# A graph and mixture-of-experts layer on one core: a wait ahead of every eighth row gather, the node stage of five groups moved into the aggregation, and the expert bias moved from the combine stage into the experts

## The chip, the cores and the metric

The kernel runs on one core of one Trainium2 chip. The metric is the device time of one execution in microseconds, as the median of several runs. It is written in Bass: every engine (PE for matmuls, DVE and ACT for elementwise work, POOL = GpSimd, SP = the sync queue) runs its own instruction list, and the lists meet only at semaphores.

## What is computed

`x` has 6250 nodes of 256 features. The kernel pads them to 49 tiles of 128 rows, in 7 groups of 7 tiles.

```python
xn = layernorm(x)
gnn = relu(xn @ W_self + (segment_sum(xn[src], dst) / max(deg, 1)) @ W_neigh + b)   # 100000 edges
mix = (linear_attention(xn) * sigmoid(gelu(norm(xn) @ Wg1 + bg1) @ Wg2 + bg2)) @ Wproj + bproj
x2 = x + gnn + mix
y = layernorm(x2)
h = y @ W_gat                                    # 4 heads x 4 experts
alpha = softmax over the 131072 edges + self loops of a node of leaky_relu(a_src[src] + a_dst[dst])
scores = layernorm(segment_sum(h[src] * alpha) + b_gat).mean(heads)
gate = softmax of the two best of four scores, else 0
out = x2 + sum_e gate[e] * (gelu(y @ W1[e] + b1[e]) @ W2[e] + b2[e])
```

## The kernel before, in words

The program has five stages, each in blocks that end with a meeting of all engines.

`prepare` normalises `x`, writes the table `xn_tab` (rows already multiplied by `W_neigh`) to DRAM, sorts the 100000 edges by target and makes tables that say for each round of the aggregation which target tile it adds to, and how far the gathers must have come.

`aggregate` sums the table rows of each target. POOL issues 784 indirect DMAs at line 857, one per 128 edges: each fetches 128 rows of 1 KB into one slot of a ring `msg` of 4 quarters with 8 slots each. Eight gathers are called a half, and there are 98 halves. POOL makes one stop in each half, ahead of its fifth gather (`u == 4`): it waits until PE has finished with the ring quarter that the next half will overwrite (`t.freed`), and until the whole previous half has landed (`landed`), which it then tells PE through the semaphore `s_landed`. ACT builds one-hot matrices `hot` (`prep`, lines 1301 and 1303). PE multiplies them with the gathered rows into 4 PSUM banks (`steps`, line 1125), two slots a round, and DVE adds each bank to `acc` (`sums`, line 879). Between these rounds the same engines do the attention branch of `mix` (PE lines 1142 to 1196) and sort the 131072 edges of the attention stage (DVE lines 218 to 273). The attention branch writes its result and the self term of `gnn` to DRAM, as `base_d`, two rows of 256 a node. The aggregation has 880 slots in all; the last 144 of them are called `rest(u0, u1)`, in PE's list and in DVE's, and hold no work of `mix` beside them. SP loads the first three groups of `base_d` back (`BASES`) during `rest`.

`gnn_out` begins when the aggregation has ended. For each unit (a group of 7 tiles, or 4 or 3 tiles of one at both ends) DVE divides the sums by the degree and adds the base (`mean`, line 1481), forms `x2` (line 1492) and its moments (lines 1496 and 1499), ACT takes the root and normalises (line 1585), PE transposes the rows (line 1635), ACT copies them out (line 1596), PE multiplies them with `w_gat` (line 1646), and SP stores `x2`, the transposed rows (`x2nT_d`) and the heads' rows (`hx_d`). The keys of the sorted edges are loaded and decoded beside it.

`gat_gather_experts` does two things side by side. POOL issues 648 indirect DMAs (line 1821) that gather the heads' rows of the sorted edges, paced by PE's progress (`paced`), with no stop for landings inside a block of 112. PE runs 4 experts on 7 groups: the first layer (line 1996) into 4 banks, which ACT puts through gelu (line 2061), and the second layer (line 2011) into 2 banks `psY`, two tiles a bank, which ACT copies out (line 2068).

`gat_combine` finds each node's sums by 49 more indirect DMAs (line 2175) and 49 small matmuls (`sel`, line 2190), computes the gates in two parts (tiles 0 to 13, then 14 to 48: `gates_of`), and for each group adds four gated expert rows and a bias: ACT scales two experts' rows (line 2225), DVE does two by a multiply and add (line 2421), adds ACT's two (line 2426), and adds the bias `gates @ b2`, which PE makes from transposed gates (lines 2201 and 2207, copied between by ACT) and DVE reads from PSUM (line 2429).

```python
for h in range(HALVES):                      # line 847, POOL
    q = h % QUART
    for u in range(SHALF):
        if h and u == SHALF // 2:
            if h + 1 in range(QUART, HALVES):
                at = h + 1 - QUART
                pool.wait_ge(s_mm, pool.value_load(t.freed[:, at:at + 1], ...))
            landed(h - 1)
        at = h * SHALF + u
        pool.indirect_dma_start(msg[:, q, u, 0:D], None, c.xn_tab, ...).then_inc(s_g[q], 16)
```

## Time and profile before

| | |
|---|---|
| median of 3 runs | 2260.66 us (2257.95 to 2261.66) |
| span of the profiled execution | 2712.5 us |
| its own time | no other figure of it is given than the span |
| mean granted TensorE clock in it | 0.825 |
| first to last gather of the aggregation (line 857) | 102.8 to 1387.9 us |
| `gnn_out` | about 1415 to 1503 us |
| first to last gather beside the experts (line 1821) | 1503.8 to 2453.3 us |
| `gat_combine` | about 2524 to 2712 us |

The profiled execution is 452 us, or 20%, longer than the median run. A row of the trace is therefore a row of an execution that ran slower than the ones that are timed; where it lost time, and where not, has to be read from the trace before its durations are summed. Times in the trace are microseconds from the start of the span; "idle" is the time an engine stood before an instruction, with what ended it; "issue" means that nothing the profile shows was waited for.

### The profile page before, as it was taken

The page shows a single profiled execution, that of the slowest core. Times are in us where ns is not written, and L with a number is a line of the kernel's source. Part 1 is how long each engine was busy: PE and PEld are TensorE (multiplying, and loading weights), DVE is VectorE, ACT ScalarE, POOL GpSimd, SP SyncE. Part 2 cuts the span into 40 slices and gives each one's busy share as a digit, 9 for nine tenths or more (in the row PEclk, how much of TensorE's full clock was granted, in tenths as well). Part 3 has the DMA queues.
Part 4 walks back from the last instruction along what each step waited for, and adds up shares of the span by engine and source line. Part 5 has one row for each costly group of instructions (what it writes and reads, how often), then busy time and mean ns, then how long its engine had stood idle before and what let it go on. Part 6 is the DMA issues. An engine that isn't in the chain of part 4 may idle for free. (4 is left out here: it accounts for less than half of the span.)

```text
span 2712.5 us, 26680 instructions
## 1 busy us (share of the span) xinstructions
PE 1935.5 (71%) x7528; PEld 1334.5 (49%) x7528; DVE 1195.4 (44%) x2204; ACT 893.4 (33%) x1910; POOL 1474.4 (54%) x1512
## 2 busy tenths in 40 slices
PE   5588778876766776666547788878888788884235
PEld 4454445454544544444336455555555565553223
DVE  6353222344454555443348433324424344256368
ACT  3433345444435343443315211321222213132124
POOL 2456456565656665556630566666666666661510
PEclk8888789887888888777775799998999889897555
DMA  5443222234334433435329511121211212215544
GB/s 182 147 132 123 62 82 86 72 117 135 117 112 130 130 118 105 131 93 179 89 61 296 208 36 50 36 70 36 70 36 50 56 45 61 51 36 172 159 148 152
DMA packets 197044, 282.80 MB, mean 104 GB/s; under 512 B 43024, under 2 KB 147443, under 8 KB 195762
## 3 DMA queue, kind: packets, MB, share of 16 engines
q0 software_dynamic: 61280, 115.13, 15.9%
q1 hardware_dynamic: 97218, 121.11, 13.5%
q10 hardware_dynamic: 38416, 44.96, 5.0%
q8 instruction: 66, 1.08, 0.2%
q14 instruction: 64, 0.52, 0.1%
HBM read 195.29 MB, written 85.80 MB: 104 GB/s over the span
## 5 line engine op out<-in xcount | busy, mean ns | idle before, releaser
L857 POOL DMA_INDIRECT ag_msg<-xn_tab,step_src x784 | 782.1, 998 | 504.9 <-issue 224.0
L1821 POOL DMA_INDIRECT edge_rows<-hx_d,gat_src x648 | 621.2, 959 | 329.6 <-issue 187.4
L1125 PE MATMUL ag_ps<-ag_msg,ag_hot 128*128 x1760 | 494.0, 430 | 113.5 <-issue 67.8
L1125 PEld LDWEIGHTS ag_ps<-ag_msg,ag_hot 128*128 128x128 f32 x1760 | 366.8, 216 | 238.5 <-issue 181.2
L879 DVE TENSOR_TENSOR acc<-acc,ag_ps 128x257 f32 x440 | 186.0, 423 | 671.1 <-remote 329.8
L2011 PE MATMUL ex_psY<-co_rows 128*128 128x256 f32 x1568 | 401.4, 413 | 100.2 <-issue 44.5
L2011 PEld LDWEIGHTS ex_psY<-co_rows 128*128 128x128 f32 x1568 | 320.8, 208 | 175.6 <-issue 68.7
L1996 PE MATMUL ex_psF<-co_rows 128*128 128x448 f32 x896 | 360.7, 557 | 42.8 <-ACT co_rows L2061 16.9
L1301 ACT ACTIVATE gat_self<-iota_row,step_nloc 128x128 f32<-128x128 f32 x880 | 271.4, 388 | 343.3 <-issue 199.1
L1935 DVE TENSOR_TENSOR hi_one_low<-hi_numbers,hi_low 128x2048 bf16<-128x2048 f32 x64 | 146.4, 2287 | 481.3 <-remote 309.5
L1996 PEld LDWEIGHTS ex_psF<-co_rows 128*128 128x128 f32 x896 | 172.2, 196 | 214.5 <-issue 187.6
L2061 ACT ACTIVATE co_rows<-ex_psF,ex_b 128x448 f32<-128x448 f32 x224 | 136.1, 633 | 247.6 <-PE ex_psF L1996 166.6
L2068 ACT COPY co_rows<-ex_psY 128x512 f32<-128x512 f32 x112 | 59.3, 532 | 473.2 <-remote 207.3
L1142 PE MATMUL mx_ps<-wqkv,xnT 128*128 128x512 f32 x196 | 105.1, 663 | 55.7 <-ACT gat_dst L1314 40.5
L1303 ACT ACTIVATE ag_hot<-gat_self,ones 128x1024 f32<-128x1024 f32 x110 | 126.3, 1148 | 13.6 <-issue 6.0
L1194 PE MATMUL mx_ps<-wself,xnT 128*128 128x256 f32 x196 | 62.4, 448 | 83.4 <-DVE xnT L903 55.4
L1936 DVE TENSOR_TENSOR hi_one_high<-hi_numbers,hi_high 128x1568 bf16<-128x1568 f32 x64 | 114.0, 1781 | 0.0
L1194 PEld LDWEIGHTS mx_ps<-wself,xnT 128*128 128x128 f32 x196 | 41.2, 219 | 95.7 <-DVE xnT L903 59.1
L1142 PEld LDWEIGHTS mx_ps<-wqkv,xnT 128*128 128x128 f32 x196 | 40.4, 211 | 89.8 <-issue 44.2
L1312 ACT ACTIVATE gat_dst<-mx_ps 128x256 f32<-128x256 f32 x49 | 18.7, 382 | 190.7 <-PE mx_ps L1145 87.9
L218 DVE TENSOR_TENSOR gatsort_keys<-gatsort_keys 128x512 f32<-128x512 f32 x117 | 80.2, 686 | 1.0
L219 DVE TENSOR_TENSOR gatsort_keys<-gatsort_keys 128x512 f32<-128x512 f32 x117 | 80.1, 685 | 0.0
(377 smaller groups left out, 2004.9 us busy)
## 6 DMA issues: line engine op xcount, KB each, us to landing
y_d<-co_rows ACTq DMA_DIRECT2D x28, 896.0 KB
co_rows<-y_d SPq DMA_DIRECT2D x28, 896.0 KB, 9.5
ag_msg<-xn_tab,step_src POOLq DMA_INDIRECT x784
xnT<-base_d SPq DMA_DIRECT2D x7, 1792.0 KB
edge_rows<-hx_d,gat_src POOLq DMA_INDIRECT x648
base_d<-xnT ACTq DMA_DIRECT2D x7, 1024.0 KB
sums_d<-edge_rows SPq DMA_DIRECT2D x5, 1344.0 KB
xg<-in_x_dram SPq DMA_DIRECT2D x7, 896.0 KB, 6.1
```

The source lines that it names most:

```text
L857: pool.indirect_dma_start(msg[:, q, u, 0:D], None, c.xn_tab, bass.IndirectOffsetOnAxis(ap=t.idx[:, at:at + 1], axis=0)).then_inc(s_g[q], 16)
L879: V.tensor_tensor(own, own, bank[(at // JOIN + u) % BANKS][:, 0:ROWW], ALU.add).then_inc(s_acc, 1)
L1125: last = nc.tensor.matmul(bank[(at + r) % BANKS][:, 0:ROWW], hot[:, k, u0 + r * JOIN + j, :], ring[:, j * ROWW:SLOTS * ROWW][:, ds(places[ ...
L1142: nc.tensor.matmul(b[:, :], xnT[:, k, at:at + P], wqkv[:, k, D:3 * D], start=(k == 0), stop=False, skip_group_check=True)
L1301: A.activation(dif[:, u, :], c.iota_row[:], ACT.Abs, bias=t.nloc[:, ds(half * SHALF + u, 1)])
L1303: A.activation(hot[:, k], dif[:], ACT.Relu, bias=c.ones[:, 0:1], scale=-1.0).then_inc(s_hot, 1)
L1821: pool.indirect_dma_start(G[:, j % RING, w, :], None, c.hx_d, bass.IndirectOffsetOnAxis(ap=plan.idx[:, at + w:at + w + 1], axis=0)).then_i ...
L1935: V.tensor_tensor(one_low[:, k % 2], bcast(numbers, 1, HIST), bcast(low[:, at], 2, P), ALU.is_equal)
L1936: V.tensor_tensor(one_high[:, k % 2], bcast(numbers[:, 0:HIGHS], 1, HIST), bcast(high[:, at], 2, HIGHS), ALU.is_equal).then_inc(s_one, 1)
L1996: last = nc.tensor.matmul(psF[i % FB][:, 0:HB], w1[:, e, k, (i % HC) * P:(i % HC + 1) * P], yT[:, k, (i // HC) * HB:(i // HC + 1) * HB], s ...
L2011: last = nc.tensor.matmul(bank[:, (u - u0) * D:(u - u0 + 1) * D], hh[:, k].rearrange("p a b -> p (a b)")[:, u * P:(u + 1) * P], w2[:, e, k ...
L2061: nc.scalar.activation(hh[:, i % HC, i // HC, :], psF[i % FB][:, 0:HB], ACT.Gelu, bias=b1[:, e * HC + i % HC:e * HC + i % HC + 1]).then_in ...
```

## The change

Four edits.

1. In the aggregation POOL gets a second stop in each half: ahead of the eighth gather it waits until the seven others of this half have landed.
2. A class `NodeRows` holds the work of `gnn_out`. Its units are all 4 or 3 tiles now. Five of the seven groups (10 units, `FUSED = 5`) are done beside `rest`: DVE does `mean` of unit i at slot 60 + 8 i and `moments` four slots later, ACT does `root`, `normed`, `turned` and `headed` between its `prep`s and behind them, PE does `turns` and `heads` between the rounds of `rest(80, ...)`, with the two banks `mix` taken in turn, and SP stores `x2`, the turned rows and the heads and loads the base groups 3 to 6. `x2` is written over `acc`, and the normalised rows over the base. `gnn_out` keeps groups 5 and 6 and the keys.
3. The combine stage computes the gates in three parts (groups 0 and 1, 2 to 4, 5 and 6), and has no transposes of gates, no bias matmuls and no third addition of DVE.
4. The bias goes into the experts instead: `b2` is loaded to all partitions (512 KB), ACT copies it into a bank of `psY` before PE's second layer adds to it, and PE waits for that copy.

```diff
@@ aggregate, SP
+                nodes.load_heads(sp, a)
...
-                    sp.dma_start(base[:, g], rows_v[:, g * GT:(g + 1) * GT, :]).then_inc(c.s_base[g], 16)
+                    nodes.base_in(sp, g)
...
                 sp.dma_start(c.skey_gat[0:P].rearrange("(p j) -> p j", p=1), first[:]).then_inc(s_out, 16)
+                nodes.rows_out(sp, 0)
+                nodes.rows_out(sp, 1)
+                nodes.base_in(sp, 3)
+                nodes.turned_out(sp, 0)
...
                 sp.dma_start(c.skey_gat[P + SORT_N:P + GAT_N].rearrange("(p j) -> p j", p=P), upper[1][:]).then_inc(s_out, 16)
+                nodes.heads_out(sp, 2)
+                nodes.base_in(sp, 6)
+                nodes.turned_out(sp, 3)
+                nodes.rows_out(sp, 4)
+                nodes.heads_out(sp, 3)
+                nodes.turned_out(sp, 4)
@@ aggregate, POOL
                             landed(h - 1)
+                        if u == SHALF - 1:
+
+                            pool.wait_ge(s_g[q], 16 * (SHALF * (h // QUART) + u))
@@ aggregate, DVE
                     sums(at, tiles_of(at, u1 - u0), 0, u1 - u0)
+                    i, begun = divmod(u1 - FINAL, SHALF)
+                    if begun == 0 and 0 <= i < FUSED_UNITS:
+                        nodes.mean(v, i)
+                    elif begun == SHALF // 2 and 0 <= i <= FUSED_UNITS:
+                        if i:
+                            nodes.scales(v, i - 1)
+                        if i < FUSED_UNITS:
+                            nodes.moments(v, i)
@@ aggregate, PE
-                rest(80, 120)
+                rest(80, 92)
+                nodes.turns(pe, 0, 0, KC)
+                rest(92, 96)
+                nodes.turns(pe, 0, KC)
+                rest(96, 104)
+                nodes.heads(pe, 0)
...
-                rest(132, REST)
+                rest(132, 136)
+                nodes.heads(pe, 2)
+                rest(136, 140)
+                nodes.turns(pe, 3, 0, KC)
+                rest(140, REST)
+                nodes.turns(pe, 3, KC)
+                nodes.heads(pe, 3)
+                nodes.turns(pe, 4)
@@ aggregate, ACT
+                    if h >= 2 * S_ITERS - BESIDE:
+                        noded(h - 2 * S_ITERS + BESIDE)
+                for i in range(BESIDE, FUSED_UNITS + 2):
+                    noded(i)
+                nodes.turned(act, FUSED - 1, KC)
@@ NodeRows
+    def base_in(self, sp, g):
+
+        if g >= BASES:
+            sp.wait_ge(self.s_x2, (g - BASES + 1) * GT)
+            sp.wait_ge(self.s_fill, (g - BASES) * self.FILLS + 2 * KC)
+        sp.dma_start(self.base[:, g % BASES], self.base_v[:, g * GT:(g + 1) * GT, :]).then_inc(self.c.s_base[g % BASES], 16)
...
+    def normed(self, act, i):
+
+        g, u0, n = self.unit(i)
+        act.wait_ge(self.s_scale, i + 1)
+        for u in range(u0, u0 + n):
+            self.c.nc.scalar.activation(self.base[:, g % BASES, u, D:2 * D], self.rows[:, g * GT + u, 0:D], ACT.Identity,
+                                        bias=self.shift[:, g % 2, u:u + 1], scale=self.rstd[:, g % 2, u:u + 1]).then_inc(self.s_y, 1)
@@ gat_gather_experts, SP, PE and ACT
+                sp.dma_start(b2[:].rearrange("p e d -> p (e d)"),
+                             a["b2"].rearrange("e d -> (e d)").rearrange("(o n) -> o n", o=1).to_broadcast([P, EXPERTS * D])).then_inc(s_w[0], 16)
...
-                        pe.wait_ge(s_yc, (g * EXPERTS + e) * len(FILLS) + f + 1)
+                        fill = (g * EXPERTS + e) * len(FILLS) + f
+                        pe.wait_ge(s_yc, max(fill + 1, 2 * fill + YB - 2))
...
-                                                        w2[:, e, k, :], start=(k == 0), stop=(k == HC - 1))
+                                                        w2[:, e, k, :], start=False, stop=(k == HC - 1), skip_group_check=True)
...
+                def biased(n, f):
+
+                    m = FILLS[f][1]
+                    nc.scalar.copy(psY[f % YB][:, 0:m * D].rearrange("p (t d) -> p t d", t=m),
+                                   bcast(b2[:, n % EXPERTS], 1, m)).then_inc(s_yc, 1)
...
                         nc.scalar.copy(yo[:, u0:u0 + m, :].rearrange("p t d -> p (t d)"), psY[f % YB][:, 0:m * D]).then_inc(s_yc, 1)
+
+                        act.wait_ge(s_yc, 2 * (n * len(FILLS) + f) + YB + 1)
+                        biased(n + (f + YB) // len(FILLS), (f + YB) % len(FILLS))
@@ gat_combine
-        CUT = 2
-        parts = [slice(0, CUT * GT), slice(CUT * GT, TILES)]
+        CUTS = (0, 2, 5, GROUPS)
+        parts = [slice(a0 * GT, a1 * GT) for a0, a1 in zip(CUTS, CUTS[1:])]
...
-                pe.wait_ge(s_in, 64)
-                for g in range(GROUPS):
-
-                    pe.wait_ge(s_exp_in, 4 if g < CUT else 7)
...
-                    last.then_inc(s_bias, 1)
...
-                        turned_gates(g)
...
                     for e in range(BY_ACT):
                         v.wait_ge(s_term, BY_ACT * g + e + 1)
-                        V.tensor_tensor(rows[EXPERTS], rows[EXPERTS], rows[e], ALU.add)
-                        v.drain()
-                    v.wait_ge(s_bias, g + 1)
-                    V.tensor_tensor(rows[EXPERTS], rows[EXPERTS], ps_b[:, 0:GT * D], ALU.add).then_inc(s_sum, 1)
+                        if e:
+                            v.drain()
+                        last = V.tensor_tensor(rows[EXPERTS], rows[EXPERTS], rows[e], ALU.add)
+                    last.then_inc(s_sum, 1)
```

## Rows read from the trace of the kernel before

**Rows 1.** POOL's three lines of gathers: duration min/median/max in ns, first and last start

```profile
L857 POOL DMA_INDIRECT ag_msg<-xn_tab,step_src x784: 940/946/2322, 102.8 to 1387.9; - x196
...
L1821 POOL DMA_INDIRECT edge_rows<-hx_d,gat_src x648: 938/944/2098, 1503.8 to 2453.3; - x162
...
L2175 POOL DMA_INDIRECT gc_num<-sums_d,gat_endpos x49: 940/944/1084, 2525.1 to 2585.2; - x49
```

**Rows 2.** Windows 2542 to 2601: busy us of each engine, TensorE clock, DMA share, GB/s

```profile
2542.00:2594.00 52.00, 4.91 (x25) 6.43 (x24) 11.55 (x44) 3.46 (x5) 33.45 (x36) 0.50 0.36 100
2594.00:2601.00 7.00, 6.78 (x32) 5.84 (x31) 6.43 (x18) 0.18 (x1) 0.00 (x0) 0.50 0.00 0
```

**Rows 3.** Timeline of 1300 to 1315: start, length, engine, [idle before it]

```profile
1300.41 0.95 POOL L857 DMA_INDIRECT ag_msg<-xn_tab,step_src  x1 [0.30 <-issue]
1301.66 0.95 POOL L857 DMA_INDIRECT ag_msg<-xn_tab,step_src  x1 [0.30 <-issue]
...
1306.48 1.12 POOL L857 DMA_INDIRECT ag_msg<-xn_tab,step_src  x1 [3.87 <-remote]
...
1313.00 0.97 POOL L857 DMA_INDIRECT ag_msg<-xn_tab,step_src  x1 [0.30 <-DMA ag_msg<-xn_tab,step_src]
```

**Rows 4.** Windows around the gather of 1301.66, same columns as rows 2

```profile
1301.66:1302.61 0.95, 0.00 (x0) 0.00 (x0) 0.00 (x0) 0.00 (x0) 0.95 (x1) 0.50 0.44 134
1302.61:1304.10 1.49, 0.00 (x0) 0.00 (x0) 0.00 (x0) 0.00 (x0) 0.00 (x0) 0.50 0.32 91
1304.10:1306.48 2.38, 1.56 (x4) 1.29 (x5) 1.20 (x3) 0.77 (x3) 0.00 (x0) 0.50 0.00 0
```

**Rows 5.** DMA queues of 1251.3 to 1256.2, behind a gather that ended at 1251.23

```profile
DMA packets 841, 1.86 MB, mean 379 GB/s; under 512 B 62, under 2 KB 62, under 8 KB 839
...
q1 hardware_dynamic: 674, 1.35, 75.9%
q0 software_dynamic: 165, 0.48, 27.0%
```

**Rows 6.** Waits of POOL, 200 to 1400: us in total, times, longest

```profile
POOL ag_msg L857 <- PE ag_ps L1125: 207.1, 42, 14.2
POOL ag_msg L857 <- issue: 206.1, 655, 3.8
POOL ag_msg L857 <- remote: 50.7, 16, 4.4
```

**Rows 7.** Windows of the stages from 1239 on, same columns as rows 2

```profile
1239.00:1389.00 150.00, 77.09 (x233) 55.25 (x232) 45.60 (x91) 49.59 (x124) 100.74 (x104) 0.70 0.40 127
...
1389.00:1415.00 26.00, 15.40 (x53) 11.24 (x51) 12.55 (x48) 2.18 (x5) 0.23 (x1) 0.73 0.10 29
1415.00:1503.00 88.00, 54.40 (x294) 52.77 (x294) 67.99 (x237) 42.76 (x94) 1.61 (x3) 0.57 0.75 241
1503.00:1516.00 13.00, 4.56 (x7) 2.35 (x8) 8.14 (x15) 1.12 (x1) 9.94 (x11) 0.51 0.95 322
1516.00:2454.00 938.00, 791.24 (x3444) 534.44 (x3443) 351.38 (x333) 222.51 (x358) 611.45 (x639) 0.92 0.21 57
```

**Rows 8.** Timeline of the first unit of `gnn_out`

```profile
1415.57 1.67 DVE L1481 SCALAR_TENSOR_TENSOR acc<-acc,go_rdeg,xnT 128x256 f32<-128x256 f32 x4
1417.33 1.43 DVE L1492 SCALAR_TENSOR_TENSOR go_x<-acc,xnT 128x256 f32<-128x256 f32 x4
1418.85 1.40 DVE L1496 BATCH_NORM_STATS2 go_stats<-go_x 128x6 f32<-128x256 f32 x4
1420.33 0.38 DVE L1499 BATCH_NORM_AGGREGATE go_mv<-go_stats 128x2 f32<-128x6 f32 x4
```

**Rows 9.** DVE's longest wait in 1415 to 1503, at the end of `gnn_out`

```profile
DVE gs_keep L1890 <- PEq L1431: 14.7, 1, 14.7
```

**Rows 10.** Groups of PE's work in 1420 to 1560: busy us, mean ns, idle

```profile
L1646 PE MATMUL go_psH<-go_wg,go_yT 128*128 128x24 f32 x196 | 34.3, 336 | 8.2 <-ACT go_yT L1596 8.2
...
L1635 PE MATMUL go_psY<-ident,go_y 128*128 128x128 f32 x98 | 21.8, 409 | 22.8 <-DVEq L1540 15.3 <-ACT go_y L1585 7.5
```

**Rows 11.** ACT's copies out of the second layer's banks, and who waited for them

```profile
L2068 ACT COPY co_rows<-ex_psY x112: 372/585/592, 1538.3 to 2464.3; 128x512 f32<-128x512 f32 x84, 128x256 f32<-128x256 f32 x28
...
  PE ex_psY L2011: 40.0, 9
```

**Rows 12.** DVE's bias additions, and pieces of the chain that ended last

```profile
L2429 DVE TENSOR_TENSOR co_rows<-co_rows,co_ps_b x7: 2020/2022/2022, 2609.4 to 2705.8; 128x1792 f32<-128x1792 f32 x7
...
2623.46 0.59 DVEq L2325
...
2647.49 1.67 PE co_ps_gT L2201 x7
2649.20 0.78 issue
```

More of the change, by code:

```diff
@@ L682, with aggregate @@
 CHUNKS = 2 * GROUPS
+FUSED = 5
 REST = S_ITERS * SBLK - 2 * R_PAIR * SBLK
[L686 removed]
+def aggregate(c, a, t, acc, plan, xnT, r2, base, nodes):
     nc = c.nc
@@ L1578, in rows @@
-                def rows(i):
-                    g, u0, n = units[i]
-                    act.wait_ge(s_scale, i + 1)
-                    if g >= 2:
-                        act.wait_ge(s_turn, (g - 1) * TURNS)
-                    for u in range(u0, u0 + n):
-                        A.activation(y[:, g % 2, u, :], x2[:, g % 2, u, :], ACT.Identity, bias=shift[:, g % 2, u:u + 1],
-                                     scale=rstd[:, g % 2, u:u + 1]).then_inc(s_y, 1)
-                def turned(g, first=0, end=TURNS):
-                    if g >= 2 and first == 0:
-                        act.wait_ge(s_yst[g % 2], 16 * (g // 2))
-                        act.wait_ge(s_hx, g - 1)
-                    for j in range(first, end):
-                        (u0, n), k = HALF[j // KC], j % KC
-                        act.wait_ge(s_turn, g * TURNS + j + 1)
-                        A.copy(yT[:, g % 2, k, u0 * P:(u0 + n) * P], psY[j][:, 0:n * P]).then_inc(s_yT, 1)
@@ L1650, in _ @@
-                pe.wait_ge(s_wg, 1)
-                for g in range(GROUPS):
-                    turns(g)
-                    heads(g)
+                nodes.heads(pe, FUSED - 1)
+                for g in range(FUSED, GROUPS):
+                    nodes.turns(pe, g)
+                    nodes.heads(pe, g)
 def gat_gather_experts(c, a, plan, hot, early, far_in):
@@ L2149, in gat_combine @@
         PER = 512 // CAR
-        FIRST = CUT * GT
-        places = [(ps_b, 0, FIRST), (ps_in, FIRST, FIRST + PER), (ps_out, FIRST + PER, TILES)]
+        edges = [0, parts[0].stop, (parts[1].start + parts[1].stop) // 2, parts[1].stop, TILES]
+        places = list(zip(ps_sel, edges, edges[1:]))
+        assert all(t1 - t0 <= PER for _, t0, t1 in places)
         def sel(t):
@@ L2322, in carried @@
                     v.wait_ge(s_sel, i + 1)
-                    for bank, t0, t1 in places[0:1] if i == 0 else places[1:]:
+                    for bank, t0, t1 in places:
+                        if not T.start <= t0 < T.stop:
+                            continue
                         V.tensor_copy(got[:, t0:t1, :], bank[:, 0:(t1 - t0) * CAR].rearrange("p (t r) -> p t r", r=CAR))
@@ L2494, in program @@
         prepare(c, a, t, acc, plan, xnT, r2)
-        aggregate(c, a, t, acc, plan, xnT, r2, base)
-        gnn_out(c, a, acc, plan, base)
+        nodes = NodeRows(c, sb, acc, plan, xnT, base)
+        aggregate(c, a, t, acc, plan, xnT, r2, base, nodes)
+        gnn_out(c, plan, nodes)
     ctx, sb, ps = c.open()
```

437 lines of the change are left out of this document (236 added, 201 removed).

## The prediction

> **What bounds the kernel now.** The first question is what the 452 us are by which the profiled execution is longer than the median. I read the windows first. In the combine stage there is a stretch of 52 us in which POOL gathers, and PE gets 25 small matmuls done; in the 7 us after POOL's last gather it does 32 of the same kind [rows 2]. Nothing in the list makes PE wait for those gathers, and "issue" is all that the trace names. So while gathers run, the profiled execution holds other engines back. I take that as a cost of being profiled, which a timed run hasn't got. Busy shares of the aggregation and the experts are then of little use, and I look for what can't be compressed.
>
> That is POOL's issue of gathers. One takes 0.946 us in the median, in all three stages [rows 1], and the next begins 0.30 us later [rows 3], so 1.25 us each. The three lines hold 784 + 648 + 49 = 1481 gathers: 1851 us. Around them, by their first and last starts [rows 1] and a last length of about 1.3 and 0.9 us, lie 102.8 us ahead of the first, 114.6 between aggregation and experts, 70.9 between experts and combine, and 126.3 behind the last. The sum is 1851 + 415 = 2266 us. The profiled execution itself took 2712.5 us, 447 more, which is POOL waiting or running long in it; but the median of the timed runs is 2260.7, within 6 us of POOL's chain with no wait at all. So my reading is that in the timed runs POOL sets the pace of the aggregation and nearly that of the experts.
>
> How much could be waiting in the runs? Of the 126 us at the end, some 36 are due to the held-back PE (the first two groups' output, 2601 to 2623, and the late selection could run beside the gathers), so about 30 us of POOL waits fit into a timed run. In the profile they are 207 us for PE and 51 for what the trace can't name [rows 6].
>
> **The wait at every eighth gather.** Only POOL's gathers stand behind it, and `landed` of this half, which PE's rounds need. Its price is the time from the end of a gather's instruction to its landing, since the next gather begins 0.30 us after either. The instruction that began at 1301.66 ends at 1302.61 and its queue moves data to 1304.10, then 0 GB/s: 1.49 us at most [rows 4]. That a landing which POOL waits for adds nothing to the 0.30 us is seen at 1313.00 [rows 3]. I take 1.4 us, and 98 halves: +137 us where POOL is the pace. The Trainium skill (Perfetto Trace Analysis, DMA Instruction — SWDGE (GPSIMD)) says that the bar of such an instruction ends when the descriptors are written, and not at the landing; by the window behind 1302.61 [rows 4] the trace agrees, and whoever took the bar's end as the landing would price this edit at 0 and the whole change at 2216 us.
>
> Below, the price is 0: POOL's waits for PE [rows 6] are 207 us, more than 137, and if the timed runs have them too, each new wait only shortens the next old one. I use that as far as the sum leaves room: of the 30 us about 20 are absorbed. Above, landings take longer beside large transfers: for 5 us the other queue holds 76% of the engines' time and the gathers 27% [rows 5]. No row gives a landing alone there; the longest stop not put down to PE is 4.4 us [rows 6], and I take that as the upper end. The aggregation's last 176 us hold 14 halves, and edit 2 puts five stores of `x2`, five of turned rows and three base loads more beside them (some 14 MB; at the 322 GB/s of the busiest window [rows 7], 44 us of full queues). A quarter of 14 halves at 3 us more is +11, all of them is +42. The Trainium skill (DMA: Bandwidth & Descriptors, Latency and other measured facts) gives the latency of HBM as 0.2 us on average and 2 us under high load. By it, an estimate, every half would cost 1.8 us more if the load were high all along, 176 us on top; the window above is at 91 GB/s [rows 4] and shows no such load, so the sum goes by the rows.
>
> This edit: 137 - 20 + 11 = +128, ends 0 and +180.
>
> **Five groups beside the aggregation.** `gnn_out` takes 88 us, with DVE busy 68 [rows 7]. A unit of four tiles costs DVE 1.67 + 1.43 + 1.40 + 0.38 = 4.9 us [rows 8], 1.25 a tile with gaps. For the two groups left, 14 tiles are 17.5 us; keys and probe some 8; and the end behind DVE's last work is 14.7 us [rows 9] and stays. That makes 40, so -48. The 35 other tiles put 44 us on DVE into 150 us where it is busy 46, and on PE 5/7 of 34.3 + 21.8 = 40 us [rows 10] where it is busy 77 of 150 [rows 7]; 35 ACT rows and copies are some 30 us beside its 50. Between gathers at 1.25 us that fits under POOL: 8 slots last 10 us or more, and DVE needs 4.9 for the unit, 1.7 for four sums and 2.8 for two sorting steps. Should that cover go, the excess is about 1 us for each of 10 units. Behind the last gather there are 26 us in which PE does its last rounds [rows 7]. Heads 1 to 3 and turns 2 to 4 stand in PE's list between or behind these, 3 x 4.9 + 3 x 3.1 = 24 us of PE, of which I take 14 as added. SP's queue gets the loads and stores too; base group 6 is asked for only after turns 3, and its 1.8 MB come in 6 us at 322 GB/s, while group 5 is worked on. Together -48 + 14 = -34; ends -48 (all hidden) and -10 (PE's 24 us and DVE's excess exposed).
>
> **Combine.** Seven additions of 2.02 us leave DVE's chain [rows 12], with their drains 14.5 us. The turn of the gates ahead of both parts, 1.67 + 0.78 us on the chain each [rows 12], goes too: 5. A third pass of `gates_of` is added: the second took from 2623.46 to 2647.49 for 35 tiles [rows 12]; its instructions are short, so I put half of a pass down to their number and not to their size: 9 to 12 us. Some 4 us come from parts that needn't wait for all 49 gathers. -13; ends -36 and 0.
>
> **Bias in the experts.** The load of 512 KB ahead of the first weights is 1.6 us at 322 GB/s [rows 7]: +2. ACT's 112 copies at 0.585 us [rows 11] add 65 us to 222 busy of 938 [rows 7], so they are hidden unless PE waits for a bank. A bank holds two tiles of 4 matmuls, and PE fills the other one meanwhile at about 0.4 us a record of which there are 16: longer than two copies. PE waited 40 us for the copy before, in nine places [rows 11]; if each doubles, +20 and up to +40. I take 0 for it. The combine edits don't touch the experts' gathers.
>
> **Sum.** 2260.7 + 128 - 34 - 13 + 2 = 2344 us.
>
> **The rivals.**
> - *POOL's stop is hidden (faster).* In the timed runs PE, ACT and DVE set the pace of the aggregation, as the 207 us [rows 6] say of the profiled one, 2.7 us a half with the 51. For it: these rows. Against it: the sum of 2266 us would be chance. It decides where POOL already waits 1.4 us a half; then 2260.7 - 45 = 2216. At half of that the change comes out near 2280, and it nets nothing where 45 of the 137 us are exposed.
> - *Landings under load.* The node groups' transfers and the new stop meet: +180 in place of +128, 2396 us. For it: the shared queues [rows 5]. Against it: only 14 of 98 halves are there.
> - *The node units are not covered.* DVE or PE becomes the bound of `rest`, because turns wait for ACT's rows, those for DVE, and rounds stand behind them in PE's list: +24 on the forecast, 2368.
> - *PE waits for the biased bank.* +40 at most, 2384, and +20 likelier.
>
> **Chances.** Forecast (2310 to 2375, with the third rival at its small end) 0.45; hidden 0.27; half hidden to a net of nothing 0.08, of which 0.05 within 0.2%; load 0.10; units uncovered or banks 0.10. A difference of 0.2% is about what this measurement can tell from none. Faster 0.29, same 0.05, slower 0.66. The range must reach into both signs to hold 8 in 10: from 2205, which takes in the hidden case, to 2400, which takes in most of the load. What is left out, some 0.15, is a larger gain in combine below and bounds that add up above. The forecast's own range is 2310 to 2375.
>
> **What would show it.** In the new profile POOL's idle ahead of the eighth gather of a half is 1.7 us in place of 0.30, 98 times, and the stop at the fifth shrinks by as much as was absorbed; first to last gather of the aggregation lengthens by less than the timed runs do, since the profiled one has old waits to give. `gnn_out` is 40 us, DVE's `sums` in `rest` keep up with POOL, the stretch from last gather to its end is about 40 us, and the last group's additions are two. The prediction is wrong if the timed runs' pace isn't POOL's: then the stop is free and only the savings show.

## The result, and the profile after

| | us, median | runs, us | beside the kernel before |
|---|---|---|---|
| before | 2261.2 | 2258.0 to 2265.1 | |
| after | 2422.3 | 2418.2 to 2430.6 | 1.0717 [1.0695, 1.0739], slower |

The changed kernel is 161 us slower; 83 us were forecast. Its profiled execution took 2430.6 us with a span of 2428.5, so it is one of the timed kind, and its spans can be set against the median. The first view is that of its three lines of gathers, as [rows 1], here with POOL's idle time ahead of them and the time from an instruction's start to its landing.

```profile
L887 POOL DMA_INDIRECT ag_msg<-xn_tab,step_src x784: 943/949/2325, 107.3 to 1358.3; - x196
...
  DMA ag_msg<-xn_tab,step_src: 251.3, 99
  issue: 210.7, 682
  PE ag_ps L1167: 0.9, 3
...
DMA to landing us min/median/max: 2.7/2.8/7.5
...
L1929 POOL DMA_INDIRECT edge_rows<-hx_d,gat_src x648: 942/947/3697, 1428.5 to 2262.5; - x162
...
L2293 POOL DMA_INDIRECT gc_num<-sums_d,gat_endpos x49: 943/947/1799, 2283.1 to 2347.8; - x49
```

POOL waits 251 us for landings, 2.5 us a time, and 0.9 us for PE in the whole aggregation, where [rows 6] had 207. The other 682 gathers begin 0.31 us after the one before. So POOL's chain alone sets this stretch. Two stops, on the timeline of POOL:

```profile
695.84 0.94 POOL L887 DMA_INDIRECT ag_msg<-xn_tab,step_src  x1 [0.30 <-issue]
698.89 0.94 POOL L887 DMA_INDIRECT ag_msg<-xn_tab,step_src  x1 [2.11 <-DMA ag_msg<-xn_tab,step_src]
...
707.98 0.95 POOL L887 DMA_INDIRECT ag_msg<-xn_tab,step_src  x1 [0.30 <-issue]
714.50 0.95 POOL L887 DMA_INDIRECT ag_msg<-xn_tab,step_src  x1 [5.56 <-DMA ag_msg<-xn_tab,step_src]
```

And the windows inside them (columns as in rows 2; DMA share and GB/s stand last):

```profile
696.78:698.28 1.50, 0.00 (x0) 0.00 (x0) 1.04 (x2) 0.00 (x0) 0.00 (x1) 1.00 0.30 90
698.28:698.89 0.61, 0.00 (x0) 0.00 (x0) 0.00 (x0) 0.00 (x0) 0.00 (x0) 1.00 0.00 0
708.93:713.90 4.97, 1.77 (x4) 0.30 (x3) 3.78 (x5) 4.87 (x11) 0.00 (x1) 0.97 1.01 290
```

The data of the first stop's last gather moves for 1.50 us, as in [rows 4], but 0.61 us more pass at 0 GB/s before POOL goes on. In the second the three loads of `xnT` that SP has just issued (L823 to L825) fill the engines (share 1.01 at 290 GB/s), and POOL waits 5.56 us in place of 2.11.

The stages by windows, as [rows 7]: aggregation, up to the experts' first gather, experts, up to the first of the last gathers, and the end.

```profile
107.30:1359.20 1251.90, 926.19 (x3199) 636.67 (x3200) 580.89 (x1171) 539.32 (x1271) 789.56 (x784) 0.85 0.41 124
1359.20:1428.50 69.30, 45.65 (x225) 41.25 (x223) 40.02 (x142) 23.71 (x56) 2.17 (x4) 0.60 0.53 173
1428.50:2263.40 834.90, 740.34 (x3541) 522.46 (x3541) 394.05 (x409) 301.84 (x493) 629.34 (x648) 0.95 0.31 82
2263.40:2283.10 19.70, 0.08 (x1) 0.08 (x2) 9.36 (x42) 4.89 (x7) 0.20 (x2) 0.50 0.06 21
2283.10:2428.50 145.40, 22.77 (x104) 21.45 (x103) 112.53 (x283) 50.12 (x114) 51.02 (x49) 0.50 0.66 207
```

Beside the trace of before that stands ahead of the prediction this reads as a gain of 284 us, since that execution took 2712.5 us. That trace was of another condition, and one of the experiments is the kernel before once more, for a trace at its own time.

### The profile page after: what moved, and what is told of

Its sections match the earlier page's. It is cut to its first block and busy times, and to the rows that moved or that the text cites. A ratio compares the mean times of both kernels' runs of the same rounds, so it can differ in the third digit from the quotient of the medians.

```text
span 2428.5 us, 26700 instructions
## 1 busy us (share of the span) xinstructions
PE 1800.5 (74%) x7381; PEld 1276.0 (53%) x7381; DVE 1197.7 (49%) x2280; ACT 957.3 (39%) x2034; POOL 1494.8 (62%) x1512
## 5 line engine op out<-in xcount | busy, mean ns | idle before, releaser
L887 POOL DMA_INDIRECT ag_msg<-xn_tab,step_src x784 | 789.6, 1007 | 462.8 <-DMA ag_msg<-xn_tab,step_src 251.3
L1929 POOL DMA_INDIRECT edge_rows<-hx_d,gat_src x648 | 629.4, 971 | 205.8 <-issue 197.3
L1167 PE MATMUL ag_ps<-ag_msg,ag_hot 128*128 x1760 | 532.7, 457 | 298.0 <-POOLq L872 287.3
L1167 PEld LDWEIGHTS ag_ps<-ag_msg,ag_hot 128*128 128x128 f32 x1760 | 389.3, 230 | 428.5 <-issue 362.5
L2104 PE MATMUL ex_psF<-co_rows 128*128 128x448 f32 x896 | 349.9, 548 | 28.0 <-DMA co_rows<-in_w_dram 14.6
L2120 PE MATMUL ex_psY<-co_rows 128*128 128x256 f32 x1568 | 344.2, 380 | 0.0
L2120 PEld LDWEIGHTS ex_psY<-co_rows 128*128 128x128 f32 x1568 | 296.5, 190 | 42.8 <-issue 3.7
L1184 PE MATMUL mx_ps<-wqkv,xnT 128*128 128x512 f32 x196 | 98.3, 626 | 0.0
L1376 ACT ACTIVATE gat_dst<-mx_ps 128x256 f32<-128x256 f32 x49 | 18.8, 384 | 157.1 <-PE mx_ps L1187 156.8
L2166 ACT COPY ex_psY<-ex_b 128x512 f32<-128x512 f32 x114 | 61.2, 537 | 17.8 <-DMA co_rows<-in_w_dram 14.3
L2293 POOL DMA_INDIRECT gc_num<-sums_d,gat_endpos x49 | 51.0, 1041 | 15.2 <-issue 15.2
```

What stands on the lines that cost most here:

```text
L887: pool.indirect_dma_start(msg[:, q, u, 0:D], None, c.xn_tab, bass.IndirectOffsetOnAxis(ap=t.idx[:, at:at + 1], axis=0)).then_inc(s_g[q], 16)
L1167: last = nc.tensor.matmul(bank[(at + r) % BANKS][:, 0:ROWW], hot[:, k, u0 + r * JOIN + j, :], ring[:, j * ROWW:SLOTS * ROWW][:, ds(places[ ...
L1184: nc.tensor.matmul(b[:, :], xnT[:, k, at:at + P], wqkv[:, k, D:3 * D], start=(k == 0), stop=False, skip_group_check=True)
L1929: pool.indirect_dma_start(G[:, j % RING, w, :], None, c.hx_d, bass.IndirectOffsetOnAxis(ap=plan.idx[:, at + w:at + w + 1], axis=0)).then_i ...
L2104: last = nc.tensor.matmul(psF[i % FB][:, 0:HB], w1[:, e, k, (i % HC) * P:(i % HC + 1) * P], yT[:, k, (i // HC) * HB:(i // HC + 1) * HB], s ...
L2120: last = nc.tensor.matmul(bank[:, (u - u0) * D:(u - u0 + 1) * D], hh[:, k].rearrange("p a b -> p (a b)")[:, u * P:(u + 1) * P], w2[:, e, k ...
```

## The experiments

A set is what ran together on one chip, with runs of the kernel before among them. The kernel before took 2246 to 2269 us in some sets and 2636 to 2727 us in others. I call these the ordinary and the held condition. One numbered chip had an ordinary and a held set, so it isn't a property of the chip. No set had both. Without this, half of the numbers below can't be read.

### Parts of the stop (held: the kernel before 2707 us)

`e1_after_no_stop` is the changed kernel without its stop, `e2_before_stop` the kernel before with it:

```diff
+if u == SHALF - 1:
+    pool.wait_ge(s_g[q], 16 * (SHALF * (h // QUART) + u))
```

> The changed kernel without the wait ahead of the eighth gather; all else of the change stays. Theory (POOL sets the pace, and each stop drains its pipeline): the 98 stops cost 221 us in the changed kernel's trace, so this runs at 2422 - 221 = 2201 us, some 60 us faster than before, and POOL's idle of the aggregation falls from 463 to some 240 us. Rival (the node groups beside the aggregation slow it, and the stop only takes the blame): it stays within 60 us of 2422.

> The kernel before with that wait alone. Theory: 2261 + 98 x 2.25 = 2482 us, a little less where the transfers beside it are fewer. Rival (the stop is dear only because of the added transfers of the node groups): near 2261 + 98 x 1.7 = 2430 or less.

`e3_before_met_wait` has at the same place a wait that has been met already, on the half before, and `e5_before_stop_6th` waits only for the first six gathers of the half, on a semaphore of their own:

```diff
+if h and u == SHALF - 1:                                   # e3
+    pool.wait_ge(s_g[(h - 1) % QUART], 16 * SHALF * ((h - 1) // QUART + 1))
...
+if u == SHALF - 1:                                         # e5
+    pool.wait_ge(s_g[h % 2], 16 * EARLY * (h // 2 + 1))
```

> The kernel before with a wait at the same place that is already met: for the landing of the half before, which POOL has waited for three gathers earlier. Theory (the price is the landing that POOL sits out): 2261 us, no change beyond 5 us. Rival (a wait instruction there makes POOL's issue lose its lead, whatever it waits for): 0.6 us and more for each of 98, 2320 us.

> The kernel before with a stop ahead of the eighth gather that waits for the first six of the half and not for all seven (the last two of a half have a semaphore of their own). Theory: a landing takes 1.48 us behind the end of the instruction and POOL goes on 0.60 us later, together 2.08; the seventh gather covers 1.25 of it, so 0.8 - 0.3 = 0.5 us a stop remain, more where the queues are full: 2261 + 50 to 90 = 2311 to 2351 us. Rival (each stop costs its 2.25 us whatever stands between): 2482 us.

| | us | ratio to before |
|---|---|---|
| e1 | 2684.5 | 0.9960 [0.9907, 1.0012] |
| e2 | 2657.9 | 0.9883 [0.9819, 0.9946] |
| e3 | 2697.3 | 0.9999 [0.9953, 1.0046] |
| e5 | 2672.3 | 0.9934 [0.9889, 0.9979] |

All four expected times missed, because they were made for 2261 us. A stop that was to cost 221 us gave 1.2% back in this set. The time shows no cost of a met wait; POOL has waits to spare in this condition, but in e3's trace the eighth gathers begin 0.30 us after the seventh, as the others do, so it is free by the trace too. In e5's trace they begin 0.80 us after it in the median, the 0.5 us a stop that its expectation worked out, yet the time didn't grow. So there was a condition to be understood first.

### The change itself, beside the same (held: before 2662 us)

`f1_after` is the changed kernel whole, `f2_after_no_stop` and `f3_before_stop` are e1 and e2 again, and `f4_before_two_stops` has the stop of e2 at `u in (SHALF // 2 - 1, SHALF - 1)`.

> The changed kernel, whole. The condition is read from the kernel before beside it: about 2261 us (the ordinary condition) or about 2707 us (that of the first set of experiments). My theory, that a stop costs about 2.25 us where GpSimd's chain sets the end and nothing where TensorE's instructions come late: 2422 us beside 2261, or between 2640 and 2670 us beside 2707 (the measured 2684 us of the same kernel without the stop, less the 1 to 2 per cent that the stop alone gave there). Rival, that the slow condition adds a like amount to every kernel: 2422 + 446 = 2868 us beside 2707.

> The changed kernel without the stop at the eighth gather. Beside a kernel before of 2261 us: 2422 - 98 x 2.26 = 2201 us if the stop is the whole of the loss and the rest of the change a gain of 60 us; 2261 us or more if the rest gives nothing and part of the loss is its own. Beside 2707 us: 2684 us, as measured before in that condition.

> The kernel before with the stop alone. Beside a kernel before of 2261 us: 2261 + 221 = 2482 us if each of the 98 stops costs the 2.26 us that stand ahead of the eighth gather in the profile of the changed kernel; 2389 us if the estimate of 1.3 us a stop was right and the rest of the change brought nothing. Beside 2707 us: 2658 us, as measured before in that condition.

> The kernel before with two stops in each half of eight gathers, at the fourth and the eighth. Beside a kernel before of 2261 us: 2261 + 2 x 221 = 2703 us if every stop costs one landing and one restart; 2482 us or little over if only the first stop of a half costs and the second meets rows that have landed. Beside 2707 us: the chain of GpSimd alone would then be 2700 us or more, so near 2750 us; no change (2658 us) if GpSimd's chain sets nothing there.

| | us | ratio to before | aggregation, us |
|---|---|---|---|
| f1 | 2617.0 | 0.9855 [0.9784, 0.9925] | 1251.0 |
| f2 | 2646.2 | 0.9971 [0.9933, 1.0009] | 1252.4 |
| f3 | 2656.8 | 0.9974 [0.9934, 1.0015] | 1242.3 |
| f4 | 2823.4 | 1.0642 [1.0566, 1.0718] | 1415.1 |

The change makes the kernel 1.5% faster here (0.8 to 2.2% by the interval): in this condition the sign of the result turns round. The stop alone gave 0.3% and nothing clear of the noise, where the first set had 1.2%. The rival of a like amount for every kernel (2868 us) is out. The aggregation with the stop lasts 1251.0 us, as in the ordinary trace (1251.9): the condition doesn't lengthen this stretch. Without the stop it lasts as long, and POOL's waits say why (f2, the lines of its aggregation's gathers):

```profile
  issue: 228.9, 714
  PE ag_ps L1164: 173.7, 40
  remote: 63.8, 20
```

The timeline of f2, first of PE, shows how that comes. POOL gathers without a break, and PE's matmuls, for which the trace names no wait, first come one at a time and then stop:

```profile
597.18 1.47 PE L1164 MATMUL ag_ps<-ag_msg,ag_hot 128*128 x6
599.05 0.38 PE L1164 MATMUL ag_ps<-ag_msg,ag_hot 128*128 x1 [0.41 <-issue]
600.48 0.38 PE L1164 MATMUL ag_ps<-ag_msg,ag_hot 128*128 x1 [1.05 <-issue]
612.53 0.87 PE L1201 MATMUL mx_ps<-xnT,wg 128*64 128x384 f32 x1 [11.67 <-DVE xnT L930]
```

POOL at the same time:

```profile
600.83 0.95 POOL L884 DMA_INDIRECT ag_msg<-xn_tab,step_src  x1 [0.30 <-issue]
602.08 0.95 POOL L884 DMA_INDIRECT ag_msg<-xn_tab,step_src  x1 [0.30 <-issue]
603.33 0.95 POOL L884 DMA_INDIRECT ag_msg<-xn_tab,step_src  x1 [0.30 <-issue]
607.90 0.95 POOL L884 DMA_INDIRECT ag_msg<-xn_tab,step_src  x1 [3.62 <-remote]
```

The wait named for PE at 612.53, on DVE, is no cause: DVE did nothing from 593.8 to 607.0 either. POOL runs out of free rows and stops at 604.28; DVE goes on 2.7 us later and PE after it. That is [rows 2] and [rows 3] again. f4 gives a price where POOL sets the pace: 172.8 us for 98 stops more, 1.76 each. Its time missed both of its expectations (near 2750 us, or 2658).

### Pause or landing, eight or sixteen (ordinary: before 2253 us)

`g1_before_pause` puts four small memsets ahead of each eighth gather in place of a wait for rows. `g2_before_stop_16` has the stop in every second half only. `g3_after_stops_all` is the changed kernel with that, and with stops in the two other strings of gathers:

```diff
+for i in range(IDLE_OPS):                                  # g1, IDLE_OPS = 4
+    pool.wait_ge(s_ids, 1 + h * IDLE_OPS + i)
+    nc.gpsimd.memset(idle[:], 0.0).then_inc(s_ids, 1)
...
+if h % 2 and u == SHALF - 1:                               # g2, g3
...
+if w % 16 == 15:                                           # g3, experts
+    pool.wait_ge(s_rows[j % 2], (rows_of[j - 2] if j >= 2 else 0) + 16 * w)
...
+if t % 8 == 7 and done:                                    # g3, last 49
+    pool.wait_ge(s_num[part], 16 * done)
```

> The kernel before with a pause of GpSimd ahead of each eighth gather that waits for no row: four small memsets of a spare tile, an estimated 2 us together (512 elements each, at the 0.84 ns an element of the 10.6 us memset of acc, and their hand-over). Where the kernel before takes 2261 us both theories give 2261 + 98 x 2 = 2457 us. Where it takes 2640 to 2710 us: if any pause in the string of gathers gives the other engines back what an unbroken string takes from them, the aggregation stretch is that of the stop, 1242 us, with no wait of GpSimd for TensorE, and the time within 1 per cent of the kernel before; if what helps is that rows have landed (fewer open transfers), the pauses are added in full, the stretch is about 1450 us and the kernel 2850 us.

> The kernel before with half as many stops, at every sixteenth gather. Where the kernel before takes 2261 us: 2261 + 49 x 2.26 = 2372 us. Where it takes 2640 to 2710 us: if the string of gathers may be eight long but not sixteen, the stalls of the free string come back and the aggregation stretch stays at some 1250 us, the time within 1 per cent of the kernel before; if sixteen are short enough, the stretch is 1242 - 49 x 2.26 = 1131 us and the time about 2550 us, 4 per cent faster than before.

> The changed kernel with its stop at each sixteenth gather only, and with stops added in the other two strings of gathers: at each sixteenth row gather of the experts' stage and at each eighth of the last 49. Where the kernel before takes 2261 us: 2422 - 49 x 2.26 + 40 x 2.26 + 5 x 2.3 = 2413 us. Where it takes 2640 to 2710 us, if unbroken strings of gathers hold TensorE back: the experts' stretch falls from 945 us towards 648 x 1.25 + 40 x 2.26 = 900 us, and from the first of the last gathers to the end it takes 145 to 155 us in place of 178; the kernel is near 2540 us. If the strings do nothing to TensorE: the experts' stretch rises to 945 + 90 = 1035 us and the end by 12 us.

Measured: g1 2456.1 (1.0883 [1.0845, 1.0922]), g2 2362.3 (1.0488 [1.0458, 1.0518]), g3 2428.4 (1.0770 [1.0731, 1.0809]). In the ordinary condition a pause of POOL is paid nearly in full, whatever it waits for. g1's four memsets keep POOL for 2.3 us (224 us busy and idle in its lines) and cost 203 in 98 places, as expected; the 49 stops of g2 cost 109 us, 2.23 each. g3 took 15 us more than the 2413 expected.

### The stop alone, the rest alone (ordinary: before 2257 us)

`i1_after_no_stop` and `i2_before_stop` are e1 and e2 once more. `i3_nodes_only` takes the diff up to and with `gnn_out` and leaves out the stop; `i4_combine_bias_only` takes its part in `gat_gather_experts` and the combine stage.

> The changed kernel without its stop. Beside a kernel before of about 2255 us: 60 us less than it (about 2195 us) if all 98 stops cost the 2.26 us seen ahead of the eighth gathers; 45 us less (2210 us), as the prediction's sum had the rest of the change, if the second half of the stops costs only the 2.0 us that stretches with stops at each eighth (1242 us) and at each sixteenth (1139 us) differ by. No change or slower if part of the loss lies in the rest. Beside 2660 us or more: within 1 per cent of the kernel before, as measured twice.

> The kernel before with the stop alone, at each eighth gather. Beside about 2255 us: 221 us more (2476 us) at 2.26 us a stop, 209 us more (2464 us) if stops at each sixteenth cost 2.23 us and the others 2.0; 128 us more (2383 us) by the prediction's term. Beside 2660 us or more: within 1.2 per cent.

> The kernel before with the five node groups beside the aggregation alone (no stop, experts and combine as before). Beside about 2255 us: 34 us less by the prediction's term (2221 us); 38 us less between the two stages and 9 to 15 us given back in the aggregation, so 25 us less (2230 us), by the stretches of the traces of kernels with and without the groups; slower if the work laid beside the aggregation delays GpSimd's gathers once no stop covers it. Beside 2660 us or more: 10 to 30 us less, hard to tell.

> The kernel before with the gates in three parts and the bias laid in the experts' banks alone. Beside about 2255 us: 11 us less by the prediction's terms (-13 + 2), 9 us less by the stretches of the traces (156.8 us from the first of the last gathers to the end against 145.4, and 2.7 us more ahead of it), so 2244 to 2246 us; no change if the bias copies hold the experts back once GpSimd runs without stops. Beside 2660 us or more: 0 to 20 us less.

| | us | ratio to before | us beside 2257.2 |
|---|---|---|---|
| i1 | 2232.9 | 0.9888 [0.9867, 0.9908] | -25 [-30, -21] |
| i2 | 2458.3 | 1.0900 [1.0870, 1.0931] | +203 [+196, +210] |
| i3 | 2246.1 | 0.9958 [0.9943, 0.9973] | -9 [-13, -6] |
| i4 | 2239.5 | 0.9921 [0.9901, 0.9942] | -18 [-22, -13] |

(The last column is the ratio less one, times 2257.2.) The stop is the whole loss (stop and rest add up to 178 us, where the change took 161 in another set). The rest gains 25 us, less than the 45 to 60 expected, and its two parts add up to it within their intervals (-9 and -18). The node groups gave less than the 25 to 34 us expected of them, combine and bias more than the 9 to 11. i1 beats both kernels: 1.1% faster than before and 7.7% faster than the changed one (0.9888 / 1.0717 = 0.923, from two sets of the ordinary condition). In the held condition it was 0.3 to 0.4% below before, within the intervals (e1, f2), and slower than the changed kernel.

### The kernel before, for its trace (ordinary)

> The kernel before itself, for its trace. If it takes about 2257 us: 1034 us from the first to the last gather of the aggregation, 102 us from there to the experts' first gather, about 834 us of experts' gathers, 17 us, and 157 us from the first of the last gathers to the end; the prediction's account of the timed run (GpSimd's chain of 1481 x 1.25 us and 415 us around it) is then right in its parts. A stretch between aggregation and experts of 107 us in place of 102 would put 22 us of saving on the node groups there. If it takes 2660 us or more: the stalled stretches of the first trace, 1287 and 951 us.

It took 2255.5 us (1.0014 [0.9994, 1.0034]) and its span was 2254.0. Its aggregation's gathers, and its stages by windows:

```profile
L857 POOL DMA_INDIRECT ag_msg<-xn_tab,step_src x784: 940/946/2262, 104.8 to 1138.3; - x196
...
  PE ag_ps L1125: 0.3, 1
```

```profile
104.80:1139.30 1034.50, 858.33 (x3104) 591.99 (x3104) 538.46 (x1016) 517.04 (x1221) 793.08 (x784) 0.90 0.47 141
1139.30:1244.10 104.80, 64.45 (x320) 60.33 (x319) 74.47 (x262) 43.19 (x94) 2.13 (x4) 0.58 0.65 205
1244.10:2080.10 836.00, 740.32 (x3541) 523.03 (x3541) 394.03 (x409) 240.61 (x379) 627.66 (x648) 0.94 0.32 82
2080.10:2097.30 17.20, 0.12 (x1) 0.09 (x2) 9.35 (x42) 4.89 (x7) 0.18 (x2) 0.50 0.07 25
2097.30:2254.00 156.70, 78.18 (x251) 57.99 (x249) 120.02 (x243) 52.86 (x116) 51.07 (x49) 0.50 0.61 192
```

POOL waits 0.3 us for PE in this stretch. Every stage can now be set beside its like (us, from such windows of each trace; the first column is the time ahead of the first gather):

| | start | aggregation | to experts | experts | to last 49 | end | span |
|---|---|---|---|---|---|---|---|
| before (j1) | 104.8 | 1034.5 | 104.8 | 836.0 | 17.2 | 156.7 | 2254.0 |
| after | 107.3 | 1251.9 | 69.3 | 834.9 | 19.7 | 145.4 | 2428.5 |
| after, no stop (i1) | 101.9 | 1041.6 | 82.3 | 831.2 | 19.7 | 145.2 | 2221.9 |
| before, stop (i2) | 102.2 | 1233.2 | 107.3 | 834.5 | 17.1 | 156.8 | 2451.1 |
| node groups (i3) | 105.9 | 1039.6 | 85.2 | 836.8 | 19.3 | 156.3 | 2243.1 |
| combine, bias (i4) | 105.9 | 1034.0 | 101.9 | 831.4 | 17.1 | 144.4 | 2234.7 |
| after, held (f1) | 107.6 | 1251.0 | 70.0 | 945.4 | 68.8 | 178.0 | 2620.8 |
| no stop, held (f2) | 107.7 | 1252.4 | 89.0 | 942.0 | 70.3 | 177.8 | 2639.2 |

### Pause and stops again (held: before 2702 us)

The kernels of g1 and g3.

> The kernel before with a pause of 2.2 us of GpSimd's own work ahead of each eighth gather, measured at 2456 us beside 2253. Beside about 2255 us again 2456 us. Beside 2660 us or more: aggregation stretch 1235 to 1245 us and the time within 1 per cent of the kernel before if any pause relieves the other engines; stretch near 1450 us if the landing of rows does it.

> The changed kernel with stops at each sixteenth gather of the aggregation and of the experts and at each eighth of the last 49, measured at 2428 us beside 2253. Beside about 2255 us again 2428 us. Beside 2660 us or more: the experts' stretch 900 to 920 us in place of 945 and 150 to 160 us from the first of the last gathers to the end in place of 178 if unbroken strings hold the other engines back; 1030 us and 190 us if they do not.

k1 took 2648.9 us, 0.9821 [0.9733, 0.9908], and k2 2638.6, 0.9783 [0.9622, 0.9943], in two runs each. k1's gathers of the aggregation:

```profile
L863 POOL DMA_INDIRECT ag_msg<-xn_tab,step_src x784: 942/946/2280, 104.8 to 1339.9; - x196
...
  PE ag_ps L1131: 0.6, 4
```

1236.1 us, against 1234.4 in the ordinary set: a pause that awaits no row keeps this stretch at its ordinary length as well as a stop does. How long an unbroken string may be follows from the same stretch in both conditions (us; rows of both kernels, as named):

| | ordinary | held |
|---|---|---|
| unbroken | 1041.6 (i1) | 1252.4 (f2) |
| sixteen | 1153.9 (g3) | 1236.4 (k2) |
| eight | 1251.9 (after) | 1251.0 (f1) |
| eight, pause (before with it) | 1234.4 (g1) | 1236.1 (k1) |

Broken at each eighth gather the stretch is no longer in the held condition, at each sixteenth 82 us longer, unbroken 211. That doesn't mean that at eight the other engines are no longer held. DVE's sums in this stretch, in f1, in f2 and in the ordinary trace of after:

```profile
DVE acc L909 <- issue: 130.7, 112, 8.0
DVE acc L909 <- remote: 50.3, 20, 6.0
```

```profile
DVE acc L906 <- remote: 225.7, 46, 13.2
...
DVE acc L906 <- issue: 114.2, 120, 8.0
```

```profile
DVE acc L909 <- issue: 14.9, 38, 0.9
```

Idle time with no cause that the trace names is 181 us in f1, 340 in f2 and 15 in after. So the pauses take about half of the holding away, and what is left fits under POOL's chain, which the same pauses lengthen. In the experts, stops at each sixteenth gather gave 976.8 us where none gave 945.4: neither of my two expectations (900 to 920, or 1030). Stops at each sixteenth cost 84 us there (918.9 in g3 against 834.9), and leave 58 of the 110 us of holding. In the last string, broken at each eighth, the end took 154.8 us in k2 and as much in g3, where the unbroken string gave 178 and 145. Two windows of 51 us from some 17 us into that string, of f1 and then of k2:

```profile
2460.40:2511.00 50.60, 4.86 (x22) 6.25 (x22) 11.48 (x44) 3.46 (x5) 33.15 (x35) 0.50 0.37 95
```

```profile
2483.00:2534.00 51.00, 9.81 (x46) 9.69 (x46) 32.21 (x82) 14.74 (x33) 32.48 (x29) 0.50 0.63 189
```

PE did 46 matmuls in place of 22 and DVE 32 us of work in place of 11, beside 29 gathers in place of 35. The granted clock is 0.50 in both, and the queues move less in the held-back one (95 GB/s against 189), so neither the clock nor full queues hold the engines back there.

## Why the prediction was right and wrong

**The bound.** Right: POOL's issue of the 1481 gathers sets the pace. In j1 POOL waits for PE 0.3 us in the aggregation and 7.6 us in the experts, and span and time are 2 us apart. But that the sum of 2266 us came within 6 us of the median was luck, because two errors cancel in it. By j1 the three strings last 1034.5 + 836.0 + 66 = 1936 us and not 1851, 1.31 us a gather: the mean gather of the aggregation is 1.01 us long, where the median of 0.946 was taken. Around them lie 318 us (104.8 + 104.8 + 17.2 + 91) and not 415, a figure from the held trace. Wrong: the step that took the 452 us for "a cost of being profiled". j1 was profiled and has none of it; e1 and i1 are one kernel, profiled in the same way, and e1 has it where i1 hasn't. [Rows 2, 3, 6] show a condition of the execution, which a timed run can have as well (2636 to 2727 us). The forecast for 2261 us didn't suffer, because I had set those waits aside. But the reading hid that the stop has a second effect, and that the sign hangs on the condition.

**The stop.** This is the step that failed, in its size: +128 forecast, about 186 to 203 measured. The aggregation grew by 217 us in the traces (210 against i1, 199 for i2 against j1), and the stop alone by 203 in the timed runs. Its three terms:
- *1.4 us a stop.* The price was "from the end of a gather's instruction to its landing", and the landing was taken as the last byte moved (1.49 us, [rows 4]). The trace counts 2.8 us from an instruction's start to its landing, so 1.85 behind its end of 0.95, and POOL goes on 0.26 later. The 81 stops without load last 2.08 us, by the gaps ahead of the eighth gathers, in place of 0.30: +1.78, 174 us in 98 places. The row at 1313.00 in [rows 3] bears on none of this: it is the second gather of its half, and the program has no wait ahead of it. That reading did little harm, since 0.26 us from a landing to the next gather is near 0.30; what failed is that the last byte was taken for the landing. The Trainium skill (DMA: Bandwidth & Descriptors, Anatomy of one DMA — SWDGE (gpsimd) path) says that a semaphore fires only when the last byte is confirmed, and puts most of a fixed 2 us down to that; by the trace there is such a time, but it is some 0.35 us behind the last byte and not most of 2. With it in the sum the term is 174 for 137, +37.
- *Landings under load, +11.* 17 stops of 98 last 3.3 to 6.5 us, 47 us above 2.08 together. I had looked for them in the last 14 halves only. Four are there; ten stand beside SP's loads of `xnT` (L823 to L825) every third or fourth half, as the one at 714.50, and three beside other transfers (halves 0, 9 and 83). i2 has 15 of them without any node group. So the rival "landings under load" had the right kind of cost in the wrong place.
- *20 us absorbed.* POOL's old waits (gaps over 0.6 us, what they have above 0.30) are 8.6 us in i1 and 2.2 in after, so 6 were absorbed. The gathers themselves are 4 us shorter in all (789.6 us busy against 793.9), which no term had. 174 + 47 - 6 - 4 = 211, and the stretches of after and i1 differ by 210.

The rival "the stop is hidden", at 0.27, is what the held condition shows: 0.9883 for the stop alone in one set, 0.9974 in another, though the time there is another one. In the ordinary condition it is out.

**The node groups.** The right mechanism: -48 for `gnn_out` and +14 behind the last gather. POOL's waits in that stretch, of before (j1), of i1 and of after:

```profile
POOL gs_first_row L1799 <- POOLq L1431: 75.1, 1, 75.1
POOL go_keys L1389 <- issue: 27.2, 1, 27.2
```

```profile
POOL go_keys L1467 <- issue: 48.8, 1, 48.8
POOL gs_first_row L1904 <- POOLq L1675: 31.0, 1, 31.0
```

```profile
POOL go_keys L1470 <- issue: 35.8, 1, 35.8
POOL gs_first_row L1907 <- POOLq L1678: 31.0, 1, 31.0
```

The stage falls from 75.1 to 31.0, -44. The end of the aggregation's block, behind the last gather, grows by 22 us without the stop and by 9 with it, so the cover is thinner than I took it when POOL runs freely. The gathers' stretch grows besides, by 5 to 7 us without the stop (1034.5 to 1039.6 and 1041.6) and by 19 with it (1233.2 to 1251.9). Of the 19, 9 are longer stops (251 us of waits for landings against 242 in i2) and 8 longer gathers (789.6 us busy against 781.5); which work of the groups does that stays open. So the rival "the node units are not covered" (+24) had a cost of nearly its size, but not by its way: DVE and PE didn't become the bound, since POOL waits 0.9 us for PE in after. Alone they gain 9 us timed and 11 by the spans where the step had 34: the two large terms held, and the missing one is the delay of the gathers and of the block's end. DVE's last wait went from 14.7 to 11.5 us [rows 9].

**Combine.** -13 forecast, -11.3 and -12.3 measured in the last column of the table. PE's busy time there falls from 78 to 23 us, but it was DVE's chain that was to count. DVE's busy time there falls by 7.5 us (120.0 to 112.5); the terms of the sum were not measured one by one.

**Bias.** 0 forecast, and the rival of a waiting PE is out: for 1500 to 2200 us of after the list of PE's waits has one line, and it isn't of the second layer's banks (a tile takes 8 matmuls of that layer and not the 4 of the prediction; its 16 a bank are right).

```profile
PE ex_psF L2104 <- ACT co_rows L2178: 13.4, 5, 6.8
```

The 40 us of [rows 11] were of the held condition. The +2 for the load of the bias isn't seen in the experts' stretch, which is 1 to 5 us shorter; why it is shorter isn't shown.

**The sum.** In the profile: +217.4 for the stretch with the stop, -35.5 to the experts, -11.3 in the end, and +3.9 for start, experts and the gap ahead of the last gathers: 174.5. The profiled execution of after is the slowest of its runs, 8 us above their median, and the kernel before took 5 us more in that set than in j1, so the medians differ by 161.

The error of 78 us is split by the medians: the rest of the change gained 25 us for a forecast of 45 (i1), which is 20, and the stop took 161 + 25 = 186 for 128, which is 58. The traces give the stop more, 210: i1's profiled execution lies 9 us under its median and that of after 8 above, which is 17 of the 24 us between them. Their terms say what kind of cost it is: 37 for the landing behind the last byte, 36 for load, and 10 for waits that weren't there to absorb. Alone the stop took 203, so stop and rest add up to 178 and not to 161; the 17 us between them are open (the 178 is from one set, the 161 from another).

## What to carry to other kernels

A wait for a DMA's landing costs the view's time from start to landing, less the instruction, plus the restart, and up to three times that under load (6.5 us for 2.1): take it from the landing row, and not from when the bytes stop. Where one engine's issue is the bound, every pause on it is added nearly whole, and what it is to cover must be worth 2 us a time. Before a profile is used to price an edit, its own time has to be set beside the median: with a fifth between them it shows another condition, and an edit can be worth -1.5% in one and +7% in the other.

## What the runs showed of the hardware

- In some executions, for whole sets of runs and also on a chip that had an ordinary set, unbroken strings of indirect gathers on GpSimd hold PE, DVE and ACT back: over 1 us between instructions that wait for nothing, then up to 13 us with none. It adds 400 to 450 us of 2255. With a pause of 2 us at each eighth gather the aggregation takes its ordinary time again (1236.1 us against 1234.4), though DVE is still held, less often; at each sixteenth about three fifths of the 211 us are gone (82 left).
- What brings the condition about is open. It was not to be chosen, and no experiment on its source was made. The Trainium skill (NOTIFIC — the notification-queue block, Overflow: three behaviours, one of which stalls the engine) says that a full queue of trace records can stall the engine that writes them. Whether that is so here no run shows, and profiled runs of the same kernel were without the condition (e1 and i1).
- Gathers are a little shorter where POOL's string is broken: 997 ns in the mean with stops (i2, 781.5 us for 784) and 1000 with pauses (g1) against 1012 without (j1, 793.1). It is why i2's stretch grew by 199 us and not by the 212 of its stops. That fewer open gathers are the cause isn't shown.
- A gather of 128 rows of 1 KB moves its last byte 1.50 us behind the end of its instruction, lands at 1.85, and POOL's next gather begins 0.26 us later (the stop at 698.89).
